# Expert choice from the logits, the softmax of the second half moved behind the last tile, and scatters in fours

## The reference

```python
logits = t @ Wg                       # t: layernorm of x, 1024 x 128; Wg: 128 x 8
probs = jax.nn.softmax(logits, axis=-1)
top_v, top_i = jax.lax.top_k(probs, 2)
top_v = top_v / (jnp.sum(top_v, axis=-1, keepdims=True) + 1e-08)
comb = jnp.zeros((T, E)).at[jnp.arange(T)[:, None], top_i].add(top_v)
for e in range(E):                    # 8 experts, 128 -> 512 -> 128
    h = jax.nn.silu(t @ W1[e]) * (t @ W3[e])
    out = out + comb[:, e:e + 1] * (h @ W2[e])
```

## Time and profile before

| what | us |
|---|---|
| median of 3 runs | 455.04 (454.76 to 455.1) |
| the profiled execution, its own time | 458.45 |
| its span, first to last instruction | 456.5 |
| TensorE busy | 381.4 |
| VectorE busy | 325.3 |
| ScalarE busy | 242.7 |
| GpSimd busy | 194.7 |

### The profile page before, as it was taken

How to read it: one execution, slowest core, us unless ns; L and a number is a source line. 1 busy time by engine, 2 the same in 40 slices (tenths; PEclk the granted TensorE clock), 3 DMA queues, 4 the chain that set the end, 5 groups by cost and what they waited for, 6 DMA issues and landing times.

```text
span 456.5 us, 8284 instructions
## 1 busy us (share of the span) xinstructions
PE 381.4 (84%) x2778; PEld 220.6 (48%) x2778; DVE 325.3 (71%) x668; ACT 242.7 (53%) x474; POOL 194.7 (43%) x252
## 2 busy tenths in 40 slices
PE   7658799999689868997996999998997789799940
PEld 3415444665356444554543544633544546567720
DVE  6765594667775799879888997899642786477632
ACT  3613455655824643466567477655784625455520
POOL 5125987725655492752518053751520023014014
PEclk9966999999999999997999799998999989899985
DMA  7572708018107107331143116310130001412112
GB/s 181 126 186 63 161 3 192 17 21 188 36 1 207 38 0 164 91 84 56 47 128 93 24 43 154 93 47 9 36 93 1 13 30 48 116 33 66 47 37 63
DMA packets 44766, 34.67 MB, mean 76 GB/s; under 512 B 5965, under 2 KB 41229, under 8 KB 44429
## 3 DMA queue, kind: packets, MB, share of 16 engines
q1 hardware_dynamic: 43701, 32.03, 27.3%
q0 software_dynamic: 1024, 2.10, 1.6%
HBM read 15.11 MB, written 7.86 MB: 50 GB/s over the span
## 4 chain that ended last, share of the span: by engine, by line
PE 50%; DVE 19%; issue 9%; ACT 7%; DMA 6%; SPq 4%; POOL 3%; POOLq 0%; DVEq 0%; ACTq 0%
PE p_sc L606 9%; PE p_misc L576 6%; DVE mx L879 5%; PE p_o L638 5%; PE p_o L625 4%; PE p_misc L507 4%; SPq L1432 4%; PE p_misc L781 3%; PE p_sc L781 3%; DMA slots_in<-qx,kx 2%; PE p_misc L533 2%; ACT probs L1188 2%; DVE xn L849 2%; PE p_o L792 2%; PE p_misc L680 2%
## 5 line engine op out<-in xcount | busy, mean ns | idle before, releaser
L879 DVE TENSOR_REDUCE mx<-p_misc 128x1 f32<-128x512 f32 x192 | 122.5, 684 | 26.1 <-PE p_misc L576 24.6
L1188 ACT ACTIVATE probs<-p_sc 128x512 f32<-128x512 f32 x192 | 104.4, 597 | 57.5 <-PE p_sc L606 56.8
L576 PE MATMUL p_misc<-kS,qS 96*128 96x512 f16 x128 | 40.9, 395 | 6.4 <-DVE mx L879 6.4
L606 PE MATMUL p_sc<-qS,kS 128*128 128x256 f16 x256 | 42.2, 284 | 3.0 <-ACT probs L1188 2.4
L1302 POOL TENSOR_SCALAR veps<-meanvar 128x2 f32<-128x2 f32 x16 | 4.0, 247 | 92.6 <-DVE meanvar L835 92.3
L1344 POOL TENSOR_TENSOR psums<-probs 128x256 f32<-128x256 f32 x32 | 24.3, 760 | 42.4 <-PE p_o L632 38.4
L638 PE MATMUL p_o<-probs,v 128*32 128x256 f32 x512 | 41.4, 402 | 0.5 <-issue 0.3
L625 PE MATMUL p_o<-probs,v 128*64 128x256 f32 x256 | 34.7, 391 | 5.1 <-ACT probs L1188 5.0
L1099 DVE TENSOR_TENSOR probs<-probs,p_sc 128x512 f32<-128x512 f32 x30 | 20.6, 687 | 25.5 <-ACT probs L1266 22.5
L1370 POOL DMA_INDIRECT probs<-slots_out,kx x16 | 15.2, 950 | 49.7 <-DMA slots_out<-probs 39.6
L606 PE MATMUL p_sc<-region 128*128 128x256 f16 x256 | 34.6, 279 | 0.9 <-DVE region L893 0.9
(11 more groups left out here) (206 smaller groups left out, 747.4 us busy)
## 6 DMA issues: line engine op xcount, KB each, us to landing
region<-kx SPq DMA_DIRECT2D x24, 256.0 KB, 3.9
v<-in_L_ffn_W_dram SPq DMA_DIRECT2D x24, 256.0 KB, 2.7
region<-qx SPq DMA_DIRECT2D x24, 128.0 KB, 3.9
slots_in<-qS SPq DMA_DIRECT2D x2, 960.0 KB, 7.1
slots_out<-probs SPq DMA_DIRECT2D x30, 64.0 KB
kS<-kS SPq DMA_DIRECT2D x1, 1664.0 KB
kS<-k_scratch SPq DMA_DIRECT2D x8, 192.0 KB
kS<-slots_in SPq DMA_DIRECT2D x6, 256.0 KB, 3.2
```

The source lines that it names most:

```text
L576: pe.matmul(ps, q[:, i * P:(i + 1) * P], k, start=True, stop=True).then_inc(full, 1)
L606: last = pe.matmul(p_sc[:, half, j * S:(j + 1) * S], k[:, kt * P:(kt + 1) * P], q, start=(i == 0), stop=(i == len(pairs) - 1))
L879: dve.tensor_reduce(mx[:, b % 2, i, h:h + 1], ps, AX_X, ALU.max).then_inc(free, 1)
L1188: act.activation(probs[:, h % 8, half * 512:(half + 1) * 512], p_sc[:, half, :], ACT.Exp, scale=(DH0 if layer == 0 else DH1) ** -0.5).then ...
```

## The change

Four edits go together.

1. `compare` reads the logits, `lg[:, 0]`, in place of the probabilities, and waits for them by itself. Exp keeps the order of the logits, so the same two experts are chosen.
2. The last five instructions of `place` become a step of their own, `weights`. In half 0 it directly follows `place`.
3. In `REST`, `route`, `shares`, `best` and `weights` of half 1 get places 31.7 to 31.73, behind the last tile's `dn` (31.6) and ahead of the second half's `mix`. `gT(1, 1)` goes from 13.86 to 15.75, behind `dn` of tile 13.
4. `send` of half 1 waits for landings once, before the third token tile, in place of before each token tile: four scatters are in flight at once. Half 0 keeps its pairs.

```diff
-        "place": 17.23, "send": 25.91, "fetch": 14.23, "gT": (19.54, 0.64), "rows": 3.88},
+        "place": 17.23, "weights": 15.2, "send": 25.91, "fetch": 14.23, "gT": (19.54, 0.64), "rows": 3.88},
...
-        (3.29, 'route', 1), (3.51, 'shares', 1), (3.63, 'compare', 1), (3.68, 'rank', 1), (4.61, 'best', 1),
+        (3.63, 'compare', 1), (3.68, 'rank', 1), (31.7, 'route', 1), (31.71, 'shares', 1), (31.72, 'best', 1), (31.73, 'weights', 1),
         (4.79, 'count', 1), (4.84, 'place', 1), (5.44, 'send', 1), (8.85, 'fetch', 1), (13.62, 'gT', 1, 0),
-        (13.86, 'gT', 1, 1), (17.72, 'gT', 1, 2), (18.76, 'gT', 1, 3), (19.42, 'pick', 0), (20.61, 'mix', 0, 0),
+        (15.75, 'gT', 1, 1), (17.72, 'gT', 1, 2), (18.76, 'gT', 1, 3), (19.42, 'pick', 0), (20.61, 'mix', 0, 0),
...
             def compare(half):
-                prob = lg[:, 3, :, :]
+                logit = lg[:, 0, :, :]
+                misc_done(dve, ("logits", 2 * half + 1))
                 for i in range(NT):
-                    this = prob[:, i, :].unsqueeze(2).broadcast_to([P, E, E])
-                    other = prob[:, i, :].unsqueeze(1).broadcast_to([P, E, E])
+                    this = logit[:, i, :].unsqueeze(2).broadcast_to([P, E, E])
+                    other = logit[:, i, :].unsqueeze(1).broadcast_to([P, E, E])
...
                 dve.tensor_scalar(expert_id[:, half, :], expert[:, :], E - 1.0, None, ALU.min).then_inc(experts_set, 1)
-                link(dve.tensor_tensor(this, slotted, wide(high), ALU.is_equal))
+
+            def weights(half):
+
+                slotted, this, other = (lg[:, i, :, :] for i in (7, 8, 1))
+                link(dve.tensor_tensor(this, slotted, slot[:, 1, :].unsqueeze(2).broadcast_to([P, NT, E]), ALU.is_equal))
                 link(dve.tensor_tensor(this, this, comb[:, :, :], ALU.mult))
                 link(dve.tensor_tensor(other, comb[:, :, :], this, ALU.subtract))
                 dve.tensor_reduce(share[:, half, 0, :], other, AX_X, ALU.add)
                 link(dve.tensor_reduce(share[:, half, 1, :], this, AX_X, ALU.add))
...
                 for i in range(NT):
-                    if half or i:
+                    if (half == 0 and i) or (half == 1 and i % 2 == 0):
                         pool.wait_ge(sent, 16 * 2 * (half * NT + i))
                     for s in range(2):
                         pool.indirect_dma_start(d_in[half], bass.IndirectOffsetOnAxis(ap=slot_id[:, half, s, i:i + 1], axis=0),
```

More of the change, by code:

```diff
@@ L255, in schedule @@
                 tokens(lambda name, n, *what: step(name, *what, n=n), i, i)
-            for name in ("route", "shares", "compare", "rank", "best", "count", "place", "send", "fetch"):
+            for name in ("route", "shares", "compare", "rank", "best", "count", "place", "weights", "send", "fetch"):
                 step(name, name, 0)
@@ L1056, in place @@
                 tiles, first, end, part = (tiles_of[:, i, :] for i in range(4))
-                pos, slotted, this, other = (lg[:, i, :, :] for i in (6, 7, 8, 1))
+                pos, slotted = (lg[:, i, :, :] for i in (6, 7))
                 high, both = slot[:, 1, :], slot[:, 2, :]
-                def wide(v):
-                    return v.unsqueeze(2).broadcast_to([P, NT, E])
                 if half == 0:
@@ L1122, in _ @@
                      "k1": keys1, "v1": values1, "q1": queries1, "oT1": heads_t1, "y1": add1, "logits": logits, "route": route, "shares": shares, "compare": compare, "rank": rank,
-                     "best": best, "place": place, "gT": taken_t, "gu": product, "hT": low, "dn": result, "mix": mix}
+                     "best": best, "place": place, "weights": weights, "gT": taken_t, "gu": product, "hT": low, "dn": result, "mix": mix}
             for kind, *at in order:
```

## The result

| kernel | median of its runs, us | own time of the profiled execution | its span |
|---|---|---|---|
| before | 454.9 (453.85 to 455.1, 4 runs) | 458.45 | 456.5 |
| changed | 450.75 (449.94 to 451.18, 4 runs) | 449.94 | 447.8 |

A forecast was written before the change was run, and what follows sets the result against it. TensorE was taken as fully busy in the tiles, leaving two holes from the second half's routing: 4.05 + 4.38 = 8.4 us, tail and first half 0, off the median 455.04 gives 446.6 us, range 445.2 to 449.8.

The forecast's parts named there:

- (e): Second half, tile 11's `result`: its wait is covered, two tiles take 5.68 instead of 10.06 us, gain 4.38 us.
- (c): `weights` out of the way: tile 5's product 3.65 us earlier, `hT` of tile 6 at 372.1 instead of 376.15.
- (f): Tail: the moved softmax chain ends at 444.7, hidden behind the gather with 1.5 us to spare; cost 0.
- (a): Selection from the logits: `compare` no longer waits for the softmax and comes 1.60 us earlier.
- (b): `best` out of the way on DVE: `place` starts 2.67 us earlier.
- hole 1: Second half's routing: PE idle 2.82 us before the count, waiting for DVE's mask; the changes gain 4.05 us here.
- the clock: PE's granted clock before the count, taken as full; at half clock `hT` of tile 6 comes up to 1.1 us later.
- (d): Four scatters at a time in the second half: fetches begin at 380.9 to 383.4 instead of 388.54.
- hole 2: Paired scatters delay fetches and tile 7's `keep`, holding tile 11's `result` and PE; tile 13 to 15 takes 10.06 us.
- The drain of (f): About 1.38 us on top of each table-changing load, per the skill; chain would end at 446.1, sum losing nothing.
- four rivals: Hole 2 only shrinks, 0.17; slow clock stays, 0.17; scatters interfere, slower than before, 0.03; mask not early, 0.05.

The follow-up runs named there:

- eight at once: The changed kernel with all eight scatters of the second half in flight, no wait between them; 451.09 us, ratio 0.9885.
- the transposes only: The kernel before with only `gT(1, 1)` moved behind the down product of tile 13; 453.81 us, ratio 0.9958.
- the selection only: The changed kernel with scatters in pairs and `gT(1, 1)` back at 13.86, against the kernel before; 453.37 us, ratio 0.9974.

## Why the prediction was wrong

**The step that failed** is the one I gave a sentence: "I take ... off the median". The profiled execution was 3.4 us above the median, and I took this as an excess that the change leaves alone. Nearly all of it was inside the hole that the change closes. Repeated, the same kernel has 7.11 instead of 10.06 us there and an own time of 454.54. So the term of the sum that was mis-sized is (e): forecast 4.38 us, measured 1.37 in a usual execution. Three smaller errors point the same way: 0.35 us in (c), 0.17 us lost between the holes, and 0.75 to 1.0 us in (f).

- **(a), (b), (c), hole 1.** The three moves came out as worked, 1.61, 2.68 and 3.66 us, and so did the clock. `hT` of tile 6 is 3.70 us earlier, not 4.05: from `hT` of tile 5 to that of tile 6 are 3.14 us, 0.74 more than a tile, and I had let 0.3 for this. My own rows had the number: 376.15 - 373.01 = 3.14. That the clock stayed full was a choice between two rows, and some luck is in it.
- **(d), the scatters.** 13.1 us to the fetches where I had 12.4, as the second group of four was ready 2.89 us after its last start and not 2.25. That isn't the price of four in flight: the first group was ready as fast as a pair (a wait of 1.53), and so were eight at once (2.25). In all eight profiles with fours an 8 KB instruction fetch (queue `q14`) begins while the last group lands, which takes 2.73 to 3.02 us; in the six others none does, and there it takes 2.25 or 2.26. No run moved that fetch. It didn't matter for the time.
- **(e), hole 2.** The term was 4.38 us, and is 7.11 - 5.30 - 0.44 = 1.37 in a usual execution (0.44 for the transposes that only left the stretch). The kernel after was right, 5.3 us as forecast; the kernel before was not. The wait for the `keep` behind the fetches, which I took for the cause, is what the first profile had on top, 2.95 us through one long landing (1.76) and the clock drop behind the stall (1.19). What is there in every profile is the wait of the transposes for the bank of tile 11's `result`, which stands behind tile 12's work on DVE. The same move of `gT(1, 1)` cures both. I had noticed the long wait, 3.98 against 1.54, and used it to bound the kernel after, but didn't ask what the kernel before is without it.
- **(f), the tail.** Costed at 0; it costs 0.75 to 1.0 us, though the chain of moved steps is hidden just as I said: DVE waits for the gather 3.06 us afterwards (1.5 forecast). I had counted the instructions, but not what fetches them.

The last instruction of `weights` begins at 434.37 and the first `mix` at 437.61 in DVE's timeline, and ACT's load doesn't even wait for `route`, whose last instruction starts after it:

```profile
430.29 1.28 ACT L1253 ACT_TABLE_LOAD   x1
```

```profile
430.73 0.19 DVE L1013 TENSOR_TENSOR kx<-kx,gs 128x32 f32<-128x32 f32 x1
431.85 0.19 DVE L1020 TENSOR_REDUCE gs<-kx 128x4 f32<-128x32 f32 x1 [0.93 <-ACT kx L1253]
...
434.37 0.17 DVE L1089 TENSOR_REDUCE kx<-kx 128x4 f32<-128x32 f32 x1
437.61 0.35 DVE L1118 SCALAR_TENSOR_TENSOR x_sb<-probs,kx,x_sb 128x128 f32<-128x128 f32 x1 [3.06 <-DMA probs<-slots_out,kx]
```

The drain of (f) doesn't show here either: from the load's start to `shares` are 1.56 us, as in the earlier trace rows.

With the terms as measured, 3.70 from hole 1 and 1.37 from hole 2 are 5.07 us against the repeated profile, and 4.90 arrive at the last `result`. The missing 0.17 is lost ahead of tile 13, whose gate/up is 3.53 us earlier; the step from tile 10 to tile 11 takes 2.53 us there and not 2.40, and what holds it I haven't traced. The tail takes 17.49 - 16.47 = 1.0 of the rest, which leaves 3.9 (4.0 with the repeated profile of the changed kernel), and the medians of that chip differ by 455.34 - 451.42 = 3.9.

None of the four rivals came. The right rival, that the hole read in one execution isn't the kernel's, was missing from the list.

**What stays open.** Why single landings of scatters were long is not settled. In the first profile of before, a 16 KB instruction fetch (I take it for PE's, which has by far the most instructions) and a smaller one run while the third pair lands (DMA queues in 381.6 to 383.4):

```profile
q8 instruction: 1, 0.02, 6.3%
q14 instruction: 1, 0.01, 1.6%
```

In the repeated profile the `q8` fetch (found between 379.56 and 379.91) falls on the third pair as well, but just after its last scatter began at 379.14, and the wait was 2.07; in the kernel with the transposes only, it came about 1.7 us after that scatter began, and the wait was 3.46. With the selection only, it began before that scatter, and the wait was 1.63. That fits the delayed `keep`, which was tested, but for the scatters it is only a coincidence in three traces; no run moved this fetch.

## What to carry to other kernels

When the profiled execution lies away from the median of the runs, don't carry a difference from one to the other: profile the kernel a second time, or look for the one wait in the trace that is unlike its neighbours, and price the kernel without it. When work leaves the stretch that you measure, take it off the gain, as it comes back behind it. A stall can have two causes, one always there and one only sometimes; ask of each hole what would hold the engine if the named releaser had been on time. And when steps are moved within a program, the points at which an engine fetches its next instructions move too; if one falls on the only transfer that the end waits for, some instructions that do nothing, placed ahead of it, can put it elsewhere.

## What the runs showed of the hardware

Instruction fetches stand among the DMA queues of the profile, and they can delay a transfer that is in flight: a 64 KB store that lands in 1.51 or 1.52 us took 2.25 to 2.65 in the seven profiles in which DVE's fetch of 8 KB fell on it, and 1.52 again when 32 memsets moved that fetch ahead by 5.6 us.

Indirect scatters from GpSimd, 64 KB each, can be eight deep in flight: the whole row of eight was done 11.2 us after the first began, against 15.4 in pairs.

In the profile of before, PE's granted clock stayed at full speed over holes of 0.93 and 1.61 us and fell to half (1.2 GHz) behind holes of 2.69 and 2.82 us; in the changed kernel it stayed full over the hole of 1.22 us. The length of the hole alone doesn't tell it: in the changed kernel's own trace the window 310 to 312 has a granted clock of 0.50, and the longest hole in the 8 us ahead of it is 1.36 us, with PE busy 0.64 of 2 us from 306 to 308.

An ACT table load took 1.28 us, the first instruction that uses its result began 1.56 us after the load's start, before and after the change, and the load did not wait for the operand of the Exp behind it (430.29 against 430.73 us).
